# Adapter attention and the first maxima of the main attention in one program of 16 turns

## The reference, cut to what matters

```python
q = apply_rope(q); k = apply_rope(k)                    # (1, 32 heads, 2048, 32)
scores = einsum('bhqd,bhkd->bhqk', q, k) / sqrt(hd)     # causal
y = einsum('bhqk,bhkd->bhqd', softmax(where(causal, scores, -inf)), v)
aqkv = einsum('btc,oc->bto', adapter_wte[None], w_attn) # 10 adapter tokens
_, ak, av = split(aqkv, 3)
ascores = einsum('bhqd,xhkd->bhqk', q, ak) / sqrt(C)
ascores = gating[0] * softmax(ascores)
y = y + einsum('bhqk,xhkd->bhqd', ascores, av)
```

## Time and profile before

| | us |
|---|---|
| median of 3 runs | 2748.28 |
| lowest, highest | 2747.68, 2761.64 |
| the profiled execution, its own time | 2752.79 |
| its span in the trace | 2751.0 |
| TensorE busy | 2493.5 (91%) |
| VectorE busy | 1657.0 (60%) |
| GpSimd busy | 1308.5 (48%) |
| ScalarE busy | 1048.0 (38%) |

### The profile page before, as it was taken

How to read it: one execution, slowest core, us unless ns; L and a number is a source line. 1 busy time by engine, 2 the same in 40 slices (tenths; PEclk the granted TensorE clock), 3 DMA queues, 4 the chain that set the end, 5 groups by cost and what they waited for, 6 DMA issues and landing times. The chain is left out here.

```text
span 2751.0 us, 40043 instructions
## 1 busy us (share of the span) xinstructions
PE 2493.5 (91%) x13407; PEld 1626.6 (59%) x13407; DVE 1657.0 (60%) x3261; ACT 1048.0 (38%) x1877; POOL 1308.5 (48%) x827
## 2 busy tenths in 40 slices
PE   6789999998758999999999999999859875999997
PEld 4667677776534444444444444444348764888885
DVE  5544555110558777777777777777526554777775
ACT  3521011111331555555555555555501111444443
POOL 4452342000432767676767666667724443333232
PEclk9999999999886999999999999999979987999998
DMA  7356655212743515151515151512356754878885
GB/s 262 108 161 192 176 167 169 93 39 63 261 131 78 134 37 134 38 133 40 131 40 132 40 127 40 120 48 55 106 190 214 162 122 175 307 284 292 306 288 179
DMA packets 231903, 397.21 MB, mean 144 GB/s; under 512 B 44540, under 2 KB 95292, under 8 KB 231620
## 3 DMA queue, kind: packets, MB, share of 16 engines
q1 hardware_dynamic: 204340, 319.62, 40.2%
q0 software_dynamic: 17152, 50.38, 5.3%
q10 hardware_dynamic: 10256, 25.21, 2.9%
HBM read 299.22 MB, written 103.76 MB: 146 GB/s over the span
## 5 line engine op out<-in xcount | busy, mean ns | idle before, releaser
L1227 ACT ACTIVATE t_prob<-t_scores_psum 128x512 f32<-128x512 f32 (+3 forms) x1280 | 610.5, 538 | 449.2 <-PE t_scores_psum L1102 242.4
L1355 POOL TENSOR_TENSOR t_two<-t_prob 128x1024 f32<-128x1024 f32 (+1 forms) x321 | 694.4, 2184 | 166.5 <-ACT t_prob L1227 103.2
L1255 DVE TENSOR_REDUCE t_part<-t_seen_psum 128x1 f32<-128x512 f32 x768 | 479.5, 683 | 146.4 <-PE t_seen_psum L1075 142.3
L1075 PE MATMUL t_seen_psum<-t_k_stack,t_q_stack 97*128 97x512 f32 (+3 forms) x1283 | 523.4, 420 | 40.1 <-DVE t_q_stack L1243 22.5
L1098 PE MATMUL t_scores_psum<-t_q_stack,t_k_stack 98*128 98x512 f32 (+3 forms) x1280 | 504.2, 405 | 8.7 <-ACT t_prob L1227 7.4
L1098 PEld LDWEIGHTS t_scores_psum<-t_q_stack,t_k_stack 98*128 98x128 f32 x1280 | 243.0, 191 | 307.8 <-ACT t_prob L1227 172.5
L1075 PEld LDWEIGHTS t_seen_psum<-t_k_stack,t_q_stack 97*128 97x128 f32 x1283 | 257.5, 201 | 92.3 <-DVE t_part L1255 37.1
L1261 DVE CUSTOM_DVE_ANT_0 t_seen_psum<-t_seen_psum,t_causal 128x128 f32<-128x128 f32 (+3 forms) x515 | 250.7, 505 | 100.5 <-PE t_seen_psum L1075 90.2
L1116 PE MATMUL t_y_acc_psum<-t_prob,t_v 128*32 128x512 f32 (+3 forms) x2576 | 302.7, 542 | 0.0
L1630 PE MATMUL acc_psum<-z_e_hi,z_x_hi 128*128 128x512 f32 x576 | 228.4, 397 | 0.0
L1632 PE MATMUL acc_psum<-z_e_hi,z_x_lo 128*128 128x512 f32 x576 | 225.4, 391 | 0.0
(11 more groups left out here) (240 smaller groups left out, 3834.0 us busy)
## 6 DMA issues: line engine op xcount, KB each, us to landing
z_raw<-in_expert_w SPq DMA_DIRECT2D x80, 512.0 KB, 5.7
z_spare<-in_expert_w SPq DMA_DIRECT2D x72, 512.0 KB, 6.0
f_w_raw<-in_wmod SPq DMA_DIRECT2D x8, 2048.0 KB, 10.3
t_q_stack<-scratch_q_hi SPq DMA_DIRECT2D x64, 256.0 KB, 4.9
t_k_stack<-scratch_k_hi SPq DMA_DIRECT2D x64, 256.0 KB, 5.2
f_w_raw<-in_w_attn SPq DMA_DIRECT2D x24, 512.0 KB, 6.1
t_inverse<-scratch_inverse SPq DMA_DIRECT2D x132, 64.0 KB, 2.0
t_y<-scratch_a_y SPq DMA_DIRECT2D x33, 256.0 KB, 4.6
```

The source lines that it names most:

```text
L1075: nc.tensor.matmul(seen[:, n % BANKS, 0:width], q_stack[par][0:SEEN, h, t0:t0 + P], k_stack[par][0:SEEN, h, c * CH:c * CH + width], start= ...
L1227: nc.scalar.activation(prob[:, step % RING, h, c0:CH], scores[:, score_bank(step, h), c0:CH], ACT.Exp, scale=1.0 / math.sqrt(D)).then_inc( ...
L1255: nc.vector.tensor_reduce(dst, seen[:, n % BANKS], AX.X, ALU.max).then_inc(seen_free, 1)
L1355: nc.gpsimd.tensor_tensor(two[:, pair % 2, heads, c0:CH], a, b, ALU.add).then_inc(two_ready, 1)
```

## The change

The separate adapter program goes; adapter attention is written anew inside *attention*, unrolled in 16 turns (TURNS) of one group and 1024 tokens each. ak and av outlive the front part, and the buffers of the adapter lie where the second group's stacks lie later (a_q, a_parts, a_weight, a_prob, a_turn, a_y, each two deep). Within a turn each engine does a share of the head: head_share cuts the 78 entries into 32 pieces, two to a turn.

In a turn t TensorE does the scores of t (only the 10 used columns of each head, 40 instead of 128), the first piece of the head, the two products of turn t - 2, the second piece, and the transposes of t - 1. The scores use one of two banks, the transposes two banks of `scores`, and both products the bank of y_acc. VectorE does maximum and subtraction of t, a piece, sum and reciprocal, a piece. ScalarE does the exponential of t, the two copies of the products of t - 2, their store (512 KB), and the copy of the transposes of t - 1. GpSimd does the multiplication with the inverse, which was VectorE's, then the addition of q for t + 2. The gating factor is multiplied into av once. GpSimd's memsets stand behind turns: the row of ones of the first stack behind turn 4, prob behind 7, two behind 10, the row of ones of the second stack at the end. SyncE loads the pair for turn t + 1, in the first turns a quarter of the stacks behind it, in turn 4 v, and the rows of negated maxima where the head has its turn entries, which is in turns 4 and 10.

The row of zeros goes with its memset: *see* now multiplies 96 rows, *score* 97. y_acc and total are cleared as before, but TensorE skips the products of steps -2 and -1. The second group's first load waits until the adapter's last store has landed and its last product is done. v[0] and v[1] change places in memory.

```diff
@@ buffers
-    SEEN, TOPS = STACK + 1, STACK + 2
+    TOPS = STACK + 1
+    TURNS, AM = G * NQ // 2, 2 * TPC * HG
+        def head_share(t, half):
+            at = [HEAD * x // (2 * TURNS) for x in (2 * t + half, 2 * t + half + 1)]
+            return range(*at) if t < TURNS else range(0)
+        a_scores = lambda t: (scores[:, 0] if t % 2 == 0 else total[:, :])[:, 0:AM * A]
+        a_turned_at = scores[:, 1:3].rearrange("p a n -> p (a n)")
@@ SyncE
+            def load_pair(t):
+                g, col = a_group(t)
+                if t >= 2:
+                    sp.wait_ge(a_q_ready, t - 1)
+                for src, dst in zip(q_parts, a_parts):
+                    sp.dma_start(dst[:, t % 2], src[g, :, col]).then_inc(a_loaded_q[t % 2], 16)
...
+            for t in range(TURNS):
+                if t + 1 < TURNS:
+                    load_pair(t + 1)
+                if 1 <= t + 1 < NQ:
+                    load_quarter(t + 1)
+                if t == NQ:
+                    sp.dma_start(v[0][:, :, :], v_d[0]).then_inc(first_loaded[NQ], 16)
+                for half in range(2):
+                    for n in head_share(t, half):
+                        entry = order[n]
+                        if entry[0] == "turn":
+                            sp.wait_ge(minus_ready, unit_of(entry) + 1)
+                            load_row(sp, entry[1] % 2, entry[2], unit_of(entry) % 2)
...
+                if (i, half, c, part) == (0, 0, 0, 0):
+                    for b in range(2):
+                        sp.wait_ge(a_stored[b], 16 * (TURNS // 2))
+                    sp.wait_ge(a_acc_ready, 2 * TURNS)
@@ TensorE
-                nc.tensor.matmul(seen[:, n % BANKS, 0:width], q_stack[par][0:SEEN, h, t0:t0 + P],
-                                 k_stack[par][0:SEEN, h, c * CH:c * CH + width], start=True, stop=True).then_inc(seen_ready, 1)
+                nc.tensor.matmul(seen[:, n % BANKS, 0:width], q_stack[par][0:STACK, h, t0:t0 + P],
+                                 k_stack[par][0:STACK, h, c * CH:c * CH + width], start=True, stop=True).then_inc(seen_ready, 1)
...
+            def a_score(t):
+                pe.wait_ge(a_q_ready, t + 1)
+                if t >= 2:
+                    pe.wait_ge(a_shifted, t - 1)
+                for j in range(2 * TPC):
+                    last = nc.tensor.matmul(a_scores(t)[:, j * HG * A:(j + 1) * HG * A], a_q[:, t % 2, j * P:(j + 1) * P],
+                                            ak[:, g].rearrange("p (h a) -> p h a", a=D)[:, :, 0:A], start=True, stop=True)
+            def a_multiply(t, x):
+                pe.wait_ge(a_turn_ready, t + 1)
+                if (t, x) == (0, 0):
+                    pe.wait_ge(a_gated, 1)
+                else:
+                    pe.wait_ge(a_y_ready, 2 * t + x)
+                nc.tensor.matmul(y_acc[:, :], av[:, a_group(t)[0]], a_turn[:, t % 2, x * CH:(x + 1) * CH],
+                                 start=True, stop=True).then_inc(a_acc_ready, 1)
...
+            for t in range(TURNS + 2):
+                if t < TURNS:
+                    a_score(t)
+                head(t, 0)
+                if t >= 2:
+                    a_multiply(t - 2, 0)
+                    a_multiply(t - 2, 1)
+                head(t, 1)
+                if 1 <= t <= TURNS:
+                    a_turn_over(t - 1)
@@ ScalarE
+            for t in range(TURNS + 2):
+                if t < TURNS:
+                    a_exp(t)
+                if t >= 2:
+                    a_keep_y(t - 2, 0)
+                    a_keep_y(t - 2, 1)
+                    a_store(t - 2)
+                if 1 <= t <= TURNS:
+                    a_keep_turned(t - 1)
@@ VectorE
-                nc.vector.memset(q_stack[b][STACK:SEEN, :, :].bitcast(F32), 0.0).then_inc(zero_rows_set, 1)
-            for n in range(HEAD):
-                advance(0, n)
+            for t in range(TURNS):
+                a_shift(t)
+                head(t, 0)
+                a_norm(t)
+                head(t, 1)
@@ GpSimd
+            a_add(0)
+            nc.gpsimd.memset(a_prob[:, :, :], 0.0).then_inc(a_cleared, 1)
+            a_add(1)
+            nc.gpsimd.tensor_scalar(av[:, :, :], av[:, :, :], gating[:, 0:1], None, ALU.mult).then_inc(a_gated, 1)
+            for t in range(TURNS):
+                a_spread(t)
+                if t + 2 < TURNS:
+                    a_add(t + 2)
+                if t == 4:
+                    one_row(0, t)
+                if t == 7:
+                    nc.gpsimd.memset(prob[:, :, :, :], 1.0).then_inc(sums_set, 1)
+                if t == 10:
+                    nc.gpsimd.memset(two[:, :, :, :], 1.0).then_inc(sums_set, 1)
+            pool.wait_ge(a_scores_ready, TURNS)
+            one_row(1, TURNS - 1)
```

More of the change, by code:

```diff
@@ L840, in attention @@
         p_hi, p_lo = p_parts
+        with ExitStack() as inner:
+            ab = lambda name, shape: inner.enter_context(nc.sbuf_tensor(f"a_{name}", shape, F32))
+            ab("filler", [P, 2 * HG * T])
+            a_y, a_turn = ab("y", [P, 2, 2 * CH]), ab("turn", [P, 2, 2 * CH])
+            a_prob, a_weight = ab("prob", [P, 2, 2 * CH]), ab("weight", [P, 2, AM, A])
+            a_top, a_total, a_inv = ab("top", [P, AM]), ab("total", [P, AM]), ab("inv", [P, 2, AM])
+            a_q, a_parts = ab("q", [P, 2, 2 * CH]), [ab(f"q_{n}", [P, 2, 2 * CH]) for n in ("hi", "lo")]
         q_stack, k_stack = [None, None], [None, None]
@@ new lines, in a_turn_over @@
+            def a_turn_over(t):
+                pe.wait_ge(a_prob_ready, t + 1)
+                if t >= 1:
+                    pe.wait_ge(a_turn_ready, t)
+                for j in range(2 * TPC):
+                    last = nc.tensor.transpose(a_turned_at[:, j * P:(j + 1) * P], a_prob[:, t % 2, j * P:(j + 1) * P], ident[:, :])
+                last.then_inc(a_turned, 1)
+            def a_multiply(t, x):
[6 more added lines that the diff above has]
+                                 start=True, stop=True).then_inc(a_acc_ready, 1)
@@ new lines, in head @@
+            def head(t, half):
+                for n in head_share(t, half):
+                    if order[n][0] == "see" and order[n][3:] == (0, 0, 0):
+                        pe.wait_ge(first_loaded[order[n][2]], LOADS - 16)
+                    advance(0, n)
+            for t in range(TURNS + 2):
[7 more added lines that the diff above has]
+                if 1 <= t <= TURNS:
+                    if t == 1:
+                        pe.wait_ge(consts_loaded, 64)
+                    a_turn_over(t - 1)
@@ L1141, in _ @@
             pe.wait_ge(first_loaded[NQ], 16)
-            pe.wait_ge(ones_set, 4)
+            pe.wait_ge(ones_set, 3)
+            pe.wait_ge(one_rows_set, 2)
             pe.wait_ge(sums_set, 2)
-            for acc, lhs in ((y_acc, v[1][:, NT - 1, 0:D]), (total, ones[:, :])):
+            for acc, lhs in ((y_acc, ones[:, :]), (total, ones[:, :])):
                 for h in range(HG):
-                    nc.tensor.matmul(acc[h * D:(h + 1) * D, :], lhs, prob[:, 0, 0], start=True, stop=False)
+                    nc.tensor.matmul(acc[h * D:(h + 1) * D, :], lhs, prob[:, 0, 0], start=True, stop=(acc is y_acc))
             def project(into, own_hi, own_lo, p_hi, p_lo):
@@ L1997, in adaln_block @@
         with semaphores(nc) as sem, ExitStack() as stage:
[L1998 to L1999 removed]
             with ExitStack() as inner:
                 plain = [inner.enter_context(nc.sbuf_tensor(n, [P, KC, T], F32)) for n in ("plain_hi", "plain_lo")]
[L2002 to L2007 removed]
+            hT = [stage.enter_context(nc.sbuf_tensor(n, [P, KC, T], F32R)) for n in ("hT_hi", "hT_lo")]
+            ak, av = (stage.enter_context(nc.sbuf_tensor(n, [P, G, P], F32)) for n in ("ak", "av"))
+            front(nc, sem, x, c, wmod, w_attn, consts, scratch("mod_raw", [6 * C]), mod_rows, hT, plain, ak, av,
+                  (q_hi, q_lo), (k_hi, k_lo), v)
         with ExitStack() as inner:
@@ L2011, in adaln_block @@
         with semaphores(nc) as sem:
-            attention(nc, sem, consts, (q_hi, q_lo), (k_hi, k_lo), v, a_y, (y_hi, y_lo), scratch("inverse", [HG, CH]), w_proj, p_parts, acc)
+            attention(nc, sem, consts, ak, av, (q_hi, q_lo), (k_hi, k_lo), v, a_y, (y_hi, y_lo), scratch("inverse", [HG, CH]), w_proj, p_parts, acc)
         with semaphores(nc) as sem:
```

251 lines of the change are left out of this document (84 added, 167 removed).

## The result

The changed kernel took 2731.66 us in the median of eight runs (2723.84 to 2740.29), against 2752.09 for the kernel before on the same chip: a ratio of 0.9913 [0.9898, 0.9928].

The account below looks back on a forecast made before the run. TensorE (91% busy) was taken to bound the kernel. Start, turns, stalls and tail summed to 155.1 us against 197.9; with 0.5 for skipped products, gain 43.3 us, new median 2705 us, range 2686 to 2731.

Parts of the forecast that it names:

- The bound and the stage: TensorE bounds the kernel; all that moves lies between adapter attention's start and the first score, 197.9 us.
- rival D: Steady part begins earlier but then stalls, for instance on second-group loads: about 2743 us, chance 0.04.
- The turn: Each of 16 turns takes 7.0 us at full clock, set by TensorE, the other engines' work hidden.
- The two stalls: Pairs of turns 6 and 12, queued behind row loads, come late: together 8.7 us, bounds 0 and 14.
- rival C: Half clock stays, a turn takes 12.5 us, stage 20 us longer than now: 2768 us, chance 0.09.
- The early term: From first load to turn 4, set by loads and GpSimd's addition: 50.6 us, bounds 46 and 60.
- The tail: Behind turn 15: last products, transposes and copies 8.3 us, then clearing matmuls 2.5 us.
- The row of zeros: Removing it from the stacks, with its memset, costs or gains 0; bounds -3 and +3 us.
- The casts: In the old setup of main attention, VectorE's casts run 3 us each beside a GpSimd memset.
- Rival B: Turn is a chain of engines waiting for each other, 9.0 us each: 2729 us, chance 0.18.
- Rival A: Loads keep ahead and nothing stalls, 16 turns of 7.0 us: 2692 us, chance 0.15.

Follow-up runs that it names:

- e1: Changed kernel with the loads of pairs 6 and 12 issued ahead of the row loads of negated maxima: 2703.69 us, ratio 0.9838.
- e2: Changed kernel with 7 and 24 extra unread matmuls in turns 5 and 11, where TensorE would stand; late pairs kept: 2717.98 us, ratio 0.9877.
- e3: Changed kernel with the loads of stack quarters 1 to 3 and v spread over turns 0 to 9: 2712.25 us, ratio 0.9859.
- e4: Kernel before the change, with only the row of zeros, its memsets and the wait for them removed: 2747.97 us, ratio 1.0004.
- f2: Changed kernel with pairs 6, 12, memsets earlier, second product behind maxima, one stack part a turn (3 to 14), constants and pair 1 before quarter 0: 2691.11 us.
- after_again: The changed kernel, unaltered, measured and profiled once more on another chip: 2725.51 us, ratio 0.9890.
- c1: Changed kernel with pairs 6 and 12 ahead of the row loads, and stack quarters 1 to 3 and v spread over turns 0 to 9: 2702.32 us.
- f1: Changed kernel with pairs 6 and 12 and memsets earlier, second product behind the maxima, one stack part a turn (3 to 14), v in 15: 2693.90 us.

## Why the prediction was right and wrong

*The bound and the stage* were right: all that moved lay ahead of the first score, and rival D, which would have had some 34 us given back in the steady part, is excluded (1872.7 us against 1872.5).

*The turn* was right within 11%: 6.2 to 6.6 us against 7.0, and TensorE's order of work set it. The groups came as priced: 1.88 for eight scores (1.98), 2.34 for GpSimd's addition (2.38), 0.74 for its multiplication (0.8), 6.92 for the memset. ScalarE was busy for 2.6 us of a turn (3.0), VectorE for 3.4 to 5.7 (4.5). Over the turns 4 to 15 this was 6.0 us on the good side.

*The two stalls* came where and why the text said, behind turns 5 and 11, by pairs queued behind the row loads. They were 1.8 and 6.1 us long, 7.9 against 8.7. That the sum fits so well is partly luck: the two were priced at 4.4 and 4.3, and 3.1 of the 4.4 were for GpSimd's memset behind the late addition, for which TensorE never waited. **This is where the forecast failed, by what it left out:** it let the turns behind a stall run at 7.0. They ran at half clock, and that cost 18.9 us in the profiled execution (e1 shows it for both stalls, e2 for the second). So the 12.1 us of the turns 4 to 15 are 18.9 - 6.0 - 0.8. The text had the doubt, as rival C, and had set its threshold in a way that hid it: it asked whether all turns run at half clock, found 11.1 us a turn to be the point from which that loses, and gave the rest no price. What came was C for part of the time, four turns of it behind two stalls; the sign that the text had named, a granted clock of 1.00 from about turn 4 on, did not come. The Trainium skill's sentence, that the half rate is what sustained work lifts (TensorE: Matmul & The Clock Gate, Part 1), agrees with these traces in so far as the half clock did end under work. My reading, that it "would end itself within a turn", was wrong: from 756.5 to 777 and from 804 to 831.6 it held on, through turns busy for 93%.

*The early term* was mis-sized, 58.6 us against 50.6, within its bounds. I had let the loads alone set it, at some 273 GB/s over the whole; in the trace they ran at 226 and 225 in turns 1 and 2, and TensorE's turns at half clock (10.6 and 10.4 busy of 11.8 and 11.1) were no shorter. I had written that its work "fits in there even partly at half clock"; e3 shows that it fits with nothing to spare, which is why thinning the loads brought 4.4 us and no more. The half-clock turn was overestimated, 12.5 against 10.2 to 11.8.

*The tail*, 13.4 against 10.8, was a term that I summed at full clock. Twice the products wait 1.1 us for ScalarE's copy of the transposes (L1156), which I had in the sum for one of the two only, and the second set of transposes (L1051) takes 1.91 us where the first takes 1.04, so half clock has come back there as well, for some 3.4 us. Timeline of after behind turn 15:

```profile
844.16 1.04 PE L1051 MATMUL t_scores_psum<-t_ident,a_prob 128*128 128x128 f32 x8
846.31 1.13 PE L1060 MATMUL t_y_acc_psum<-a_turn,av 128*128 128x512 f32 x2 [1.11 <-ACT a_turn L1156]
...
849.61 1.91 PE L1051 MATMUL t_scores_psum<-t_ident,a_prob 128*128 128x128 f32 x8
```

*The row of zeros* at nothing was right as far as e4 can tell (1.0004, give or take 0.0025). *The casts*, 3.02 us beside GpSimd's memset before, take 0.23 in after. *Rival B* fell: full-clock turns without a stall were never 9 us long. *Rival A*, 2692 us, is what the kernel becomes once SyncE's order is mended and TensorE's second product moved: f2 measured 2691, with shorter turns and a longer start than A had. That e1, with the stalls gone, measured 2703.7 against a forecast of 2705 that still had them, is a balance of errors and no confirmation: -5.8 for the turns and -8.7 for the stalls, against +8.3 for the start of turn 4 (58.9 us after its first load), +2.4 for that turn's clock and, as in after, +2.6 for the tail.

What stays open is why the clock is lost for a longer or shorter time in the first four turns. The same kernel had turns 1 to 3 of 12.2, 11.8 and 11.1 us in one execution and of 14.0, 13.9 and 10.0 in another (after_again), and no run here holds it still. In the first two of these turns the difference is not the clock, 0.50 in both, but the loads, which came at 190 and 187 GB/s instead of 226 and 225 at the same DMA share of 1.06; why, no run shows. Open is also why the half clock behind much the same stand in turn 5 lasted 20.5 us in the one and 6.8 in the other. How much of the spread between the runs of one kernel this makes, I can't say from single traces.

## What to carry to other kernels

A stall of TensorE has two prices, the wait and the half clock behind it; here 7.9 us of waiting cost 18.9 more in the trace of after, so each late load is worth a line in the sum of its own, with the turns behind it priced at half rate. In a queue that issues in order, a load that is wanted soon must stand ahead of an entry that waits for another engine: three lines of order (e1) gave as much again as the whole change. And loads that are moved out of one crowded stretch should be strewn thinly, for two parts a turn made TensorE stand for a late pair three times (c1), where one a turn made it stand once, for 0.73 us (f1).

## What the runs showed of the hardware

Behind a stand of TensorE of only 1.55 us, in a turn with 6.05 us busy of 8.46, the clock went to 0.50, and it came back some 20.5 us later, though TensorE was busy for 93% of the two turns that follow; from its fall in the stand of 5.8 us it took some 27. It can be much shorter: 6.8 us behind a stand of 1.60 in another execution of the same kernel (after_again), and 3.4 behind one of 0.73 (f1). Waits of 0.81 and 0.78 us for ScalarE's copy left it at 1.00 (after, turns 9 and 10). With the stand filled (e2, turn 11) it stayed at 1.00. A cast of 128x128 on VectorE that took 0.23 us alone took 3.02 and 6.50 beside a GpSimd memset, each time until the memset was through (before, e4). In two executions of one kernel the same loads ran at 226 and at 190 GB/s, both times with a DMA share of 1.06 (after and after_again, turn 1).
